# Idle products on TensorE moved to a tile of their own and given more places, and the order of the work on all engines laid out anew, with the one-hot tables next to the ranks

## What is computed

```python
# 1: adjacency from the context
Q, K = ctx @ Wq.T, ctx @ Wk.T
sim = Q @ K.T / (sqrt(32) * 4)                  # 512 x 512 for each batch
mask = sim >= 153rd largest of its row
A = sigmoid(sim) * mask;  A = (A + A.T) / 2
x = x + tanh(g0) * ((1 - gamma) * layernorm(x) + gamma * A)
# 2: mixture of 8 experts, 2 for each token
h = layernorm(x);  two best experts by softmax(h @ gate_w)
out_e = gelu(h @ fc1[e] + b1[e]) @ fc2[e] + b2[e]
x = x + tanh(g1) * sum over the two of share * alpha[e] * out_e
```

## Time and profile before

| | us |
|---|---|
| median of 3 runs (lowest to highest) | 366.69 (365.43 to 367.62) |
| the profiled execution | 365.13 |
| its span in the profile | 363.4 |
| TensorE busy | 324.3 (89%) |
| VectorE, ScalarE, GpSimd busy | 200.7, 165.0, 100.1 |
| mean granted TensorE clock | 0.958 |

### The profile page before, as it was taken

How to read it: one execution, slowest core, us unless ns; L and a number is a source line. 1 busy time by engine, 2 the same in 40 slices (tenths; PEclk the granted TensorE clock), 3 DMA queues, 4 the chain that set the end, 5 groups by cost and what they waited for, 6 DMA issues and landing times.

```text
span 363.4 us, 6131 instructions
## 1 busy us (share of the span) xinstructions
PE 324.3 (89%) x1937; PEld 232.9 (64%) x1937; DVE 200.7 (55%) x697; ACT 165.0 (45%) x384; POOL 100.1 (28%) x141
## 2 busy tenths in 40 slices
PE   6906899779998999899999989999999999999960
PEld 4402667677764786678778576777785877577610
DVE  0488698887879777898886372636206112311010
ACT  2485515389996746256786222232222213132320
POOL 5001001361111357114307431331733111312031
PEclk9975699899999999999999999999999999999996
DMA  2999989977974696876627587744678854533253
GB/s 91 379 392 369 352 298 331 378 267 139 305 145 123 144 243 231 146 161 183 113 54 181 191 173 135 211 100 81 203 163 149 176 119 104 111 64 87 30 74 46
DMA packets 53636, 65.79 MB, mean 181 GB/s; under 512 B 9792, under 2 KB 28512, under 8 KB 53600
## 3 DMA queue, kind: packets, MB, share of 16 engines
q1 hardware_dynamic: 46144, 47.99, 43.7%
q0 software_dynamic: 7456, 17.37, 24.7%
HBM read 39.56 MB, written 25.78 MB: 180 GB/s over the span
## 4 chain that ended last, share of the span: by engine, by line
PE 50%; issue 18%; DVE 14%; DVEq 5%; DMA 5%; POOL 3%; POOLq 2%; ACT 2%; ACTq 0%
PE ps L1711 21%; PE ps L1684 13%; PE ps L1694 10%; DMA out_rows<-ab,dst 3%; PE ps L1647 2%; POOL xs_rows L566 2%; DMA meta<-xs_rows 2%; DVE top L1087 1%; DVE stats L1012 1%; PE ps L1607 1%; PE ps L1721 1%; PE ps L1627 1%; PE ps L1639 1%; POOLq L530 1%; DVEq L1086 1%
## 5 line engine op out<-in xcount | busy, mean ns | idle before, releaser
L1684 PEld LDWEIGHTS ps<-xgT_r,weights 128*128 128x128 f32 x768 | 87.8, 192 | 8.3 <-issue 6.7
L1684 PE MATMUL ps<-xgT_r,weights 128*128 128x128 f32 x768 | 89.6, 276 | 3.6 <-ACT xgT_r L743 2.0
L1711 PE MATMUL ps<-weights,act_r 128*128 128x512 f32 x192 | 86.3, 595 | 1.5 <-ACT act_r L766 1.5
L580 POOL DMA_INDIRECT out_rows<-ys,dst x24 | 37.9, 1578 | 115.2 <-ACT ys L773 70.0
L1711 PEld LDWEIGHTS ps<-weights,act_r 128*128 128x128 f32 x192 | 34.9, 190 | 38.4 <-issue 36.5
L766 ACT ACTIVATE act_r<-ps,b1T 128x128 f32<-128x128 f32 x96 | 27.1, 365 | 38.9 <-PE ps L1684 38.8
L1694 PEld LDWEIGHTS ps<-sim,weights 128*128 128x128 f32 x256 | 35.2, 190 | 1.9 <-issue 1.7
L566 POOL DMA_INDIRECT xs_rows<-ab,pos x32 | 31.9, 998 | 14.5 <-issue 9.1
L1694 PE MATMUL ps<-sim,weights 128*128 128x160 f32 x256 | 35.6, 299 | 0.0
L773 ACT ACTIVATE ys<-ys,meta 128x512 f32<-128x512 f32 x24 | 17.3, 719 | 31.3 <-DVE ys L1322 31.3
L1322 DVE TENSOR_TENSOR ys<-ps,b_r 128x512 f32<-128x512 f32 x24 | 16.5, 686 | 23.4 <-PE ps L1711 22.0
(11 more groups left out here) (206 smaller groups left out, 419.0 us busy)
## 6 DMA issues: line engine op xcount, KB each, us to landing
weights<-in_L_ffn_fc_w SPq DMA_DIRECT2D x16, 1024.0 KB, 8.0
b_r<-in_L_ffn_fc_b SPq DMA_DIRECT2D x32, 256.0 KB, 4.1
xg_r<-xs_rows SPq DMA_DIRECT2D x88, 64.0 KB
xb<-in_x SPq DMA_DIRECT2D x4, 1024.0 KB, 7.1
out_rows<-xb SPq DMA_DIRECT2D x4, 1024.0 KB, 5.5
sim<-xs_rows SPq DMA_DIRECT2D x32, 80.0 KB
xs_rows<-weights SPq DMA_DIRECT2D x1, 2064.0 KB, 13.5
xs_rows<-weights SPq DMA_DIRECT2D x2, 516.0 KB, 5.9
```

Source lines behind the costliest of these rows:

```text
L580: pool.indirect_dma_start(out=out_rows, out_offset=bass.IndirectOffsetOnAxis(ap=dst[:, k % 2, e:e + 1], axis=0), in_=result_rows(m), in_of ...
L1684: mm = pe.matmul(ps[:, n % 2, i * P:(i + 1) * P], weights[:, e, 0, h, i * P:(i + 1) * P], rows[:, h * P:(h + 1) * P], start=(h == 0), stop ...
L1711: mm = pe.matmul(ps[:, 2 + m % 2, :], rows, weights[:, e, 1, i, :], start=(i == 0), stop=(i == IB - 1))
```

## The change

1. A new tile `warm` (128 x 128 bfloat16) is set to one by VectorE and announced by a semaphore `warm_ok`. TensorE waits for it first, makes 36 idle products (before 24), and only then waits for `consts`. All idle products use `warm` in place of `ones_b`.
2. Further idle products: 8 ahead of `project(0)`, 8 behind it, 8 ahead of `adjacency(0, 0)`, and 28 in place of 16 between the adjacencies of batch 0.
3. The lists of all five engines are laid out anew. Among the moves: `one_hot(0)` stands right behind `gaps(0)`, ahead of `shares` and of `x_var(1)`; `project(3)` ahead of the picks; steps of batch 1's search earlier than parts of batch 0; the scatters of batches 2 and 3 with an `add_result` in the middle; rows of batches 1 to 3 loaded before their side data (`meta`); `load_weights(7)` later.

```diff
-BUSY_LOADS, BUSY_SEARCH, BUSY_MASK = 24, 36, 48
+BUSY_LOADS, BUSY_SEARCH, BUSY_MASK = 36, 36, 48
...
+        warm = sb("warm", [P, P], BF16)
...
-                if e == 0:
+                if e == 0 or n == PICKED:
                     sp.wait_ge(scat[k], 16 * BT * PICKS)
...
+            dve.memset(warm[:], 1.0).then_inc(warm_ok, 1)
             coefficients()
             x_stats(0, 0)
...
-                        pe.matmul(ps[:, 3, 0:P], ones_b[:], ones_b[:], start=True, stop=True)
+                        pe.matmul(ps[:, 3, 0:P], warm[:], warm[:], start=True, stop=True)
...
+            pe.wait_ge(warm_ok, 1)
+            keep_busy(BUSY_LOADS)
             pe.wait_ge(consts, 2)
-            keep_busy(BUSY_LOADS)
             pe.wait_ge(qk_in, 32)
             pe.matmul(ps[:, 0, 0:C], wq, wk, start=True, stop=True).then_inc(m_ps, 1)
             turn_context(0)
             pe.wait_ge(m_sb, 1)
+            keep_busy(8)
             project(0)
-            for t in range(BT):
+            keep_busy(8)
+            for t in range(3):
                 scores(0, t)
+            turn_context(1)
+            scores(0, 3)
+            project(1)
             turn_b1()
             sum_gate()
-            turn_context(1)
-            project(1)
+            scores(1, 0)
             turn_context(2)
-            scores(1, 0)
...
             layer1(0, 0)
             layer1(0, 1)
             layer2(0, 0)
+            layer2(0, 1)
             layer1(0, 2)
-            layer2(0, 1)
...
             layer2(3, 3)
             tails(0)
...
-            layer1(3, 6)
+            layer2(3, 6)
             layer1(3, 7)
-            layer2(3, 6)
```

More of the change, by code:

```diff
@@ L484, in _ @@
             load_b2(3, 5)
+            load_rows(3, 7)
             load_b2(3, 6)
@@ L787, in _ @@
             context(0)
+            query(0)
             tanh_coefs()
-            query(0)
             for t in range(BT):
                 scores(0, t)
-            for t in range(BT):
-                squash(0, t)
-            keep_b1()
-            signs(0, 0)
+            context(1)
+            signs(0, 0)
+            squash(0, 0)
+            squash(0, 1)
+            signs(0, 1)
+            keep_b1()
+            query(1)
+            scores(1, 0)
+            signs(0, 2)
+            squash(0, 2)
+            squash(0, 3)
             halve(0, 0)
+            for t in range(3):
+                candidates(0, t)
+            affine_x(0, 0)
             halve(0, 1)
-            signs(0, 1)
+            affine_x(0, 1)
+            scores(1, 1)
+            candidates(0, 3)
             halve(0, 2)
             halve(0, 3)
[L801 to L809, removed]
+            scores(1, 2)
+            affine_x(0, 2)
+            affine_x(0, 3)
+            scores(1, 3)
             context(2)
-            scores(1, 3)
             query(2)
@@ L818, in _ @@
             norm_plain(3)
-            scores(2, 0)
-            scores(2, 1)
+            context(3)
             leaning(0)
+            query(3)
             scores(2, 2)
[L823 to L827, removed]
             signs(1, 0)
             picked(0)
+            signs(1, 1)
+            affine_x(1, 0)
+            scores(2, 3)
             picked(1)
-            signs(1, 1)
+            affine_x(1, 1)
@@ L891, in _ @@
-            turned(2, 1)
-            turned(2, 2)
             signs(3, 2)
+            gelu(1, 3)
             weigh(1, 2)
-            turned(2, 3)
-            for t in range(BT):
-                candidates(3, t)
-            gelu(1, 3)
+            leaning(2)
+            candidates(3, 0)
+            gelu(1, 4)
+            candidates(3, 1)
+            candidates(3, 2)
+            weigh(1, 3)
+            affine_x(3, 0)
+            candidates(3, 3)
+            gelu(1, 5)
+            affine_x(3, 1)
@@ L1440, in _ @@
                 mask(2, t)
[L1441 to L1455 removed]
+            total(2, 0)
+            turn_rows(1, 0)
@@ new lines, in _ @@
+            total(2, 1)
+            total(2, 2)
+            total(2, 3)
+            sim_stats(3, 1)
+            turn_rows(1, 1)
+            sim_stats(3, 2)
+            add_bias(6)
+            add(2, 0)
+            add(2, 1)
+            turn_rows(1, 2)
+            sim_stats(3, 3)
+            add(2, 2)
+            first_guess(3)
+            add(2, 3)
+            add_bias(7)
+            x1_stats(2, 0)
+            targets(1)
+            x1_stats(2, 1)
+            turn_rows(1, 3)
+            narrow(3, 0)
@@ L1456, in _ @@
+            x_stats(3, 0)
+            turn_rows(1, 4)
+            add_bias(8)
+            x1_stats(2, 2)
+            x1_stats(2, 3)
+            x1_var_of(2)
+            narrow(3, 1)
             x_stats(3, 1)
             x_stats(3, 2)
+            norm_bias(2)
+            norm(2, 0)
             x_stats(3, 3)
-            add_bias(8)
-            add(2, 2)
-            narrow(3, 0)
+            add_bias(9)
+            turn_rows(1, 5)
             x_var(3)
-            add_bias(9)
-            add(2, 3)
@@ L1465, in _ @@
-            for t in range(BT):
-                x1_stats(2, t)
-            x1_var_of(2)
-            narrow(3, 1)
-            norm_bias(2)
-            for t in range(BT):
-                norm(2, t)
-            turn_rows(1, 4)
+            norm(2, 1)
+            best_two(2)
+            gaps(2)
             add_bias(10)
             narrow(3, 2)
+            shares(2)
             x_scales(3)
-            largest(3, 0)
-            largest(3, 1)
-            best_two(2)
-            gaps(2)
@@ L1805, in _ @@
             layer2(0, 3)
-            for t in range(BT):
-                adjacency(1, t)
+            adjacency(1, 0)
+            adjacency(1, 1)
             layer2(0, 4)
+            adjacency(1, 2)
+            adjacency(1, 3)
             turn(1, 0)
```

484 lines of the change are left out of this document (252 added, 232 removed).

## The result

The changed kernel takes 378.01 us (median of 3, 376.12 to 379.85), the kernel before 366.69 (365.43 to 367.62): a ratio of 1.031, 95% interval 1.022 to 1.041. The forecast was 366.3, range 362.0 to 370.6. The profiled execution's span is 376.3 us, before 363.4: 12.9 more.

The account below looks back on a forecast made before the run. Up to 79 us a VectorE and ScalarE chain sets the pace, then TensorE is full, then three serial stores. Terms 5.6 − 0.2 + 1.3 − 3.1 − 3.2 − 0.8 = −0.4 gave 366.3 us, range 362 to 370.6.

Parts of the forecast that it names:

- Step 1: Start: idle products wait for VectorE's late `warm` MEMSET, first guess at 23.4 us instead of 17.82; +5.6 us.
- Step 2: Search to mask: six `bn_stats` instead of five, +0.68; prove(0) no longer behind a half-rate score, −0.8; −0.2 us.
- Step 3: Mask to `member`: two `bn_stats` more, a longer norm_bias wait, one norm less before best_two; +1.3 us.
- Step 4: Picks and first layers: one-hot table sooner after `member`, but ScalarE's chain stands in front; −3.1 us.
- Step 5: Full stretch of TensorE's layers: new orders remove three quarters of at most 4.2 us of idle; −3.2 us.
- Step 6: Tail: layer2(3,6) now precedes layer1(3,7), so its store starts 4 us earlier; −0.8 us.
- Rival B: Start: the clock does not rise before the scores; +4.0 us, 370.3 in all; chance 0.13.
- Rival C: First layers: ScalarE's fixed order eats the gain of Step 4; +3.1 us, 369.4 in all; chance 0.12.
- the ring of two result buffers: Within Step 5: adds through two result buffers, one every 5.6 us at best, found ahead everywhere; no separate size.
- Rival D: Full stretch: the small idles are only moved; +3.2 us, 369.5 in all; chance 0.08.

Follow-up runs that it names:

- b_w7late: The kernel before with only `load_weights(7)` moved, to behind `load_b2(0, 3)`: 364.65 us, ratio 1.000.
- a_start: The changed kernel with the memset of `warm` ahead of VectorE's wait for the constants: 369.74 us, ratio 1.010.
- a_back3: The changed kernel with `load_weights(7)`, `add_bias(3)` and `fill_ends()` put back at their old places: 377.15 us, ratio 1.034.
- a_q3: The changed kernel with `load_weights(7)` and `add_bias(3)` back at their old places and `load_x(3)` ahead of rows (1,0): 371.07 us, ratio 1.019.
- a_w7: The changed kernel with only `load_weights(7)` back at its old place, right behind `load_x(2)`: 373.28 us, ratio 1.016.
- a_x3: The changed kernel with `load_x(3)` moved behind `load_b2(0, 5)`, ahead of rows (1,0): 375.30 us, ratio 1.027.
- a_t12: The changed kernel with VectorE's `turn_rows(1, 2)` moved behind `add(2, 3)`, no transfer moved: 375.72 us, ratio 1.029.

## Why the prediction was wrong

By its own terms, in the profiled executions. The shift after steps 1 to 4 is read at layer1(0,2): before it started at 89.22 with 3.43 us of layer2(0,1) still to do, now at 97.12 with that done, +4.5 us.

| step | forecast | measured | read from |
|---|---|---|---|
| 1, start | +5.6 | +4.7 | first guess at 22.52, before 17.82 |
| 2, search to mask | −0.2 | −0.4 | mask(0) at 49.40, before 45.08: +4.3 in all |
| 3, mask to member | +1.3 | +3.2 | `member` at 69.24, before 61.74: +7.5 in all |
| 4, picks and first layers | −3.1 | −3.0 | layer1(0,2), +4.5 in all |
| 5, full stretch | −3.2 | +9.2 | the tails' products at 361.79, before 346.81: +15.0 in all, less 1.34 of step 6 |
| 6, tail | −0.8 | −0.8 | +12.9 at the end |

The 1.34 us are TensorE's wait for the Gelu no longer covered, ahead of the tails' products, which the forecast had put at 1.4 and into step 6.

**Step 1 was right.** The ones were written late; first product 9.68 (forecast 9.5), first score 16.78 (17.55), first guess 22.52 (23.4). The full rate was there at the context's transposes at 13.71, 1.3 us sooner than the 15 that I took: 0.60 us for the four, where before they took 1.06, then 1.12 for the projection's two products and 3.00 for six score products. That is most of the 0.9 us by which the step was smaller, and within the bound that the forecast gave for it. Rival B fell: in every run with the new idle products whose trace is kept here the scores ran at the full rate. With the old start the variation that the Trainium skill (TensorE: Matmul & The Clock Gate, What's actually happening) warns of does reach them: eight score products took 6.28 us in the kernel before and 5.49 in `b_w7late`, alike up to there. That the term is a cost was shown by `a_start` (8.3 us with the gain of an early start in it).

**Step 3 was mis-sized** by 1.9 us. The forecast said that the added idle products stand where TensorE waits for VectorE, and would cost 0.07 us each were that cover gone. It was gone for the 28 between the adjacencies: VectorE's wait there grew from 0.22 to 1.95 us, 1.7 of the 1.9. In the traces of all eleven kernels with 28 it is 1.84 us or more, with 16 at most 0.22; a run with these alone taken back was not made. Step 2 was right, though its two terms, +0.68 and −0.8, make −0.1 and not −0.2. **Step 4 was right**: layer2(0,0) at 90.15 (forecast 89.4), layer1(0,2) at 97.12 (96). Rival C fell. **Step 6 was right.**

**Step 5 failed, and with it the forecast.** Its first half held: of the idles that it named, 3.4 us in all, 0.5 us is left after 200 us and nothing between 140 and 177. But two sentences were wrong. "I followed the ring of two result buffers (an add every 5.6 us at best) ... and found it ahead everywhere": I used the median landing for a store issued within 10 us of 5 MB of bulk transfers; it took 13.2 us, not about 5. And "The weights moved back (`load_weights(7)`) are needed 50 us after they are asked for and take 8": they were no trouble for their own reader, and took 17.3 and 18.2; the trouble was the reader of another transfer beside them. In the order lists I had looked at what each moved instruction waits for on engines, and not at which DMA it waits for and which transfers are under way with it. The same mistake twice more: `turn_rows(1, 2)` behind `load_x(3)` (4.1 us), and rows (0,4) in `a_back3`.

Rival D, small idles only moved (chance 0.08), was nearest in kind, but priced at 3.2 us where one wait took 5.1 and carried a further cost. The range ended at 370.6, since every bound of step 5 was made from idles of before; a wait that the new order could make had no bound at all. The nearest row for it was there, in the trace of the kernel before: the fill of 2 MB landed in 13.5 us.

**How much of step 5 is shown.** Loss between first layers and tail: +9.2. With weights, x of batch 3 and `add_bias(3)` moved, the profile of `a_q3` has the tails' products at 353.05 and layer1(0,2) at 97.88, so step 5 is −0.3 there (+6.2 less +5.2 less 1.3) in place of +9.2. But that execution was the shortest of its four (369.06 to 373.57); by the ratios, 1.031 to 1.019, the three moves give back some 4.5 us. The two readings stand side by side: between a half and all of step 5's loss over the kernel before is shown to be these waits. What is left in the profile of `a_q3` is 3.4 us at the lower clock and 1.2 of idle between 120 and 160 us, where the forecast had a gain. Why this clock falls in `a_q3` after small idles, and not in the kernel before after 0.98 us at 113, was not tried.

## What to carry to other kernels

When an order is laid out anew, list for each in-order engine the instructions that wait for a DMA, and what is queued behind each of them; then put the landing time under load there, not the median. A transfer with a far deadline is not free: it makes its neighbours late, and one of those may have an engine and a row of work standing behind it. And undo such a layout in pieces only with care: old transfers under a new order can be worse than either.

## What was unexpected of the hardware

- The landing of an accumulating store depends on what else is in flight: 4.4 to 13.2 us in one execution, with the transfer engines' share at 1.04 while the longest was out. The same store took 13.2, 11.8, 10.8 and 10.4 us in four programs alike up to there, 9.1 and 7.2 with the fill but without the weights beside it (`a_q3`, `a_w7`), 5.3 with both earlier (`a_back3`). A bulk fill of 2,064 KB took 13.5 us before and 15.2 after, the two loads of weights beside it 17.3 and 18.2, where the median of all 16 is 8.0. The Trainium skill (DMA: Bandwidth & Descriptors, Queues, rings and completion order) says that each DMA engine takes turns between the queues that have work, packet by packet. The trace agrees in so far as the store, issued last, landed at 124.0, before the weights issued at 107.05 and 108.95 (124.4 and 127.2); but its time was 2.7 times the median.
- Idle products in a loop are not all of one length: at the full clock 48 took 3.60 us, 28 took 3.75 and 76 took 6.22 (0.075, 0.134 and 0.082 us each). Twice, the 28 and the 76, they lasted longer than the wait that they stood in, and held the step behind them.
- Executions differ in whether the clock falls for a while behind the same 2.2 us wait at layer2(0,0): 1.7 us lost there in the profile of `a_x3`, none in those of the changed kernel and `a_t12`, all three alike up to there (of the others, `a_w7` and `a_start` lost it, `a_q3` did not). That is as much as several of the terms above, and it bears on single profiles.
